# State-space stage of a four-layer network on one core: step sizes replicated over the states by DMA through DRAM instead of TensorE, inputs' replicas three pairs deep, joint product with B

## The chip, the core and the metric

One core of a Trainium2 chip runs the whole program. Its engines are TensorE (PE in the profile; PEld is its weight load), VectorE (DVE), ScalarE (ACT), GpSimd (POOL) and SyncE (SP), which here only issues DMAs. SBUF has 128 partitions, PSUM 8 banks of 512 f32 columns; 16 DMA engines move data between DRAM and SBUF. The metric is the device time of one execution in microseconds, lower is better.

## The reference

The network has four layers on x of shape (16, 32, 128, 128), f32. The change concerns layer 1, a deformable convolution whose offsets pass through a state-space model ("mamba"), forward and backward over sequences of length L = 128 x 128, for 9 offsets per image:

```
def selective_scan(u, dt, A, Bm, Cm, D):
    dA = jnp.exp(dt[..., None] * A)
    dBu = dt[..., None] * Bm[:, :, None, :] * u[..., None]

    def comb(e1, e2):
        a1, b1 = e1
        a2, b2 = e2
        return (a2 * a1, a2 * b1 + b2)
    _, h = jax.lax.associative_scan(comb, (dA, dBu), axis=1)
    return jnp.einsum('bldn,bln->bld', h, Cm) + u * D
```

Here u has 18 inner channels (D_IN), h 16 states per channel (D_STATE), dt is the softplus of a projection, Bm and Cm are projections of u that all channels share. The result is gated with silu(z) and projected back to 9 rows.

## The kernel before

`program` runs the layers one behind another, each in its own block with its own buffers. `state_space` (L738) works on chunks of 512 time steps (LC). The sequence of one direction and one half of the batch (8 images) is 32 chunks long (NC), so there are N = 128 chunks, i = 0 to 127, one behind another; two buffers alternate (u = i % 2). In a chunk the 18 channels go in 9 pairs, p = 0 to 8. One channel of 8 images with 16 states fills 128 partitions.

For each pair the engines do this:

- PE replicates the step sizes dt (tile `dts`, index 0: 8 rows per channel) over the 16 states with a selection matrix `sl`, into `pr` (`rates_of`, L891), and likewise dt * u (`dts`, index 1) into `pu` (`inputs_of`, L897). Both use 32 rows of the array, the quadrant and half of a channel given by `place` (L724).
- ACT makes the decays `da` = exp(dt * A) from `pr` (`decays`, L1060). `da` has three pairs of buffers; decays run two pairs ahead of the scans.
- DVE multiplies `pu` with B in place (`inputs_by_b`, L1131, one instruction for each channel) and scans: h = da * h + pu, into `hs` (`scans`, L1140). Twice per chunk it adds the skip term (`skip`, L1151).
- POOL keeps the last column as the next chunk's carry and multiplies `hs` with C into `hc` (`outputs`, L1187).
- PE sums `hc` over the states into `py` (`reduce`, L930, and `reduce_previous`, L942).

Between the pairs of chunk i the projections of chunk i + 1 are made: PE writes them into the single bank `pp` (x, z, dt, B, C, and the previous output), ACT takes each out (`gate_x`, `gate_z`, `softplus_parts`, `softplus_logs`, `b_copy`, `c_copy`, `out_copy`). POOL makes the step sizes of chunk i + 1 in `steps` (L1174), the first half (pairs 0 to 4) behind its pair 5 and the second (pairs 5 to 8) behind its pair 7.

The order on each engine is written out by hand, and each engine runs its queue in order. In `replicate` (L916) PE waits for two things before it issues anything: scans two pairs back (`wait_inputs`, L904; `pu` has two pairs of banks) and the decays of the pair ahead (`wait_rates`, L910; `pr` has one pair of banks). Then come the inputs of pair p + 1 and the rates of pair p + 2. SP runs a loop over the chunks (L843): loads of the sequence chunk after next (`load`, six transfers of 72, 24, 48, 48, 24 and 72 rows of 2 KB), the two small tables `al` (`load_rates`), and the store of 72 rows (`store`).

Of the kernel before, what the change touches and what calls it, by code (L numbers as in the profile page):

```python
# [8 lines left out]
P = 128  # L9
# [728 lines left out]
def state_space(nc, seq, w_x, w_z, conv_rows, conv_b, w_dt, dt_rows, dt_b, w_b, w_c, a_log, keeps, d_skip, w_out,  # L738
# [5 lines left out]
    KEEP = D_IN  # L744
    USES = 9
    X0, Z0, X1, Z1, DT0, DT1, BB, CC, OUT = range(USES)
    LAST_OF = {0: 1, 1: 1, 2: 3, 3: 3, 4: 4, 5: 6, 6: 6, 7: 8, 8: 8}

    with ExitStack() as ctx:
# [24 lines left out]
        bs = m.sb("bs", [NB, 2, LC])  # L774
        cs = m.sb("cs", [NB, 2, LC])
        da = m.sb("da", [NB, 3, 2, LC])
        hs = m.sb("hs", [NB, 3, 2, LC])
# [6 lines left out]
        py = m.bank("py")  # L784
        pr = m.bank("pr", 2)
        pu = m.bank("pu", 4)
        (w_load, w_ready, a_exp, a_ready, pp_full, pp_drained, ab, e3, lg_ready, dt_ready, dtu_ready,
         rates_done, inputs_done, exp_done, dbu_done, scan_done, carry_ready, hc_done, y_done, y1_done, y2_done) = (m.sem(n) for n in (
             "w_load w_ready a_exp a_ready pp_full pp_drained ab e3 lg_ready dt_ready dtu_ready "
             "rates_done inputs_done exp_done dbu_done scan_done carry_ready hc_done y_done y1_done y2_done").split())  # L790
        s_in = [m.sem("s_in0"), m.sem("s_in1")]
        a_in = [m.sem("a_in0"), m.sem("a_in1")]
        stored = [m.sem("stored0"), m.sem("stored1")]
        LOADS = 16 * len(TAP_PARTS)
# [15 lines left out]
        def _(sp):  # L810
# [32 lines left out]
            with sp.Fori(0, N // 2 - 1) as j:  # L843
                for u in range(2):
                    chunk(j * 2 + u, j, u, False)
            store(N - 2, 0, use_of(N - 1, OUT))
            store(N - 1, 1, use_of(N, 0))
            store(N, 0, use_of(N, 1))
# [4 lines left out]
        def _(pe):  # L853
# [36 lines left out]

            def rates_of(i, u, p, part):  # L891
                hf, q, run = place(2 * p + part)
                rows = slice(32 * q, 32 * q + 32)
                pe.matmul(pr[:, LC * part:LC * (part + 1)], sl[rows, run, :], dts[rows, u, hf, 0, :],  # L894
                          start=True, stop=True, tile_position=(32 * q, 0)).then_inc(rates_done, 1)

            def inputs_of(i, u, p, part):  # L897
                hf, q, run = place(2 * p + part)
                rows = slice(32 * q, 32 * q + 32)
                bank = 2 * ((u + p) % 2) + part  # L900
                pe.matmul(pu[:, LC * bank:LC * (bank + 1)], sl[rows, run, :], dts[rows, u, hf, 1, :],  # L901
                          start=True, stop=True, tile_position=(32 * q, 0)).then_inc(inputs_done, 1)

            def wait_inputs(i, p):  # L904

                if p in (0, HALF_PAIRS):
                    pe.wait_ge(dtu_ready, i * 2 + (1 + p // HALF_PAIRS))
                pe.wait_ge(scan_done, i * D_IN + (2 * p + 4))

            def wait_rates(i, p):  # L910

                if p in (0, HALF_PAIRS):
                    pe.wait_ge(dt_ready, i * 2 + (1 + p // HALF_PAIRS))
                pe.wait_ge(exp_done, i * D_IN + (2 * p + 2))

            def replicate(i, u, p, last):  # L916

                ahead = [(i, u, p + k) if p + k < PAIRS else (i + 1, 1 - u, p + k - PAIRS) for k in (1, 2)]
                if not (last and p + 1 >= PAIRS):
                    wait_inputs(ahead[0][0], ahead[0][2])  # L920
                if not (last and p + 2 >= PAIRS):
                    wait_rates(ahead[1][0], ahead[1][2])
                for part in range(2):
                    if not (last and p + 1 >= PAIRS):
                        inputs_of(*ahead[0], part)
                for part in range(2):
                    if not (last and p + 2 >= PAIRS):
                        rates_of(*ahead[1], part)

# [31 lines left out]
            c_proj(0, 0, 2)  # L961
            wait_inputs(0, 0)
            wait_rates(0, 0)
            for part in range(2):
                inputs_of(0, 0, 0, part)
            for part in range(2):
                rates_of(0, 0, 0, part)
            wait_rates(0, 1)
            for part in range(2):
                rates_of(0, 0, 1, part)  # L970

# [39 lines left out]
        def _(act):  # L1011
# [47 lines left out]

            def decays(i, u, p):  # L1060
# [18 lines left out]
            c_copy(0, 0, False, 2)  # L1079
            decays(0, 0, 0)  # L1080
            decays(0, 0, 1)

            def chunk(i, j, u, last):
                n, un, jn = i + 1, 1 - u, j + u
                for p in range(PAIRS):
                    if p + 2 < PAIRS:
                        decays(i, u, p + 2)
                    elif not last:
                        decays(n, un, p + 2 - PAIRS)
                    if not last:  # L1090
# [24 lines left out]
        def _(dve):  # L1115
# [15 lines left out]
            def inputs_by_b(i, u, p):  # L1131
                if p == 0:
                    dve.wait_ge(pp_drained, use_of(i, BB) + 1)
                dve.wait_ge(inputs_done, i * D_IN + (2 * p + 2))
                for part in range(2):
                    bank = 2 * ((u + p) % 2) + part
                    tile = pu[:, LC * bank:LC * (bank + 1)]
                    dve.tensor_tensor(tile, tile, bs[:, u, :], ALU.mult).then_inc(dbu_done, 1)  # L1138

            def scans(i, u, p):  # L1140
# [4 lines left out]
                for part in range(2):  # L1145
                    bank = 2 * ((u + p) % 2) + part
# [1758 lines left out]
```

## Time and profile before

| | us |
|---|---|
| median of 3 runs | 20,994.22 |
| lowest, highest run | 20,714.11, 21,013.87 |
| the profiled execution | 20,821.64 |
| its span, first to last instruction | 20,820.1 |
| busy in the span: PE, DVE, ACT, POOL | 16,358.0, 14,027.1, 12,953.3, 9,553.7 |
| mean granted TensorE clock, share of full speed | 0.855 |

All rows come from the profiled execution. A group of instructions has its line, engine, operation, the tile written and the tiles read, then busy us and mean ns of one, then the engine's idle time just before them with what ended it. In the timeline each row starts with start and duration in us; "x2" are two instructions run together. A DMA queue's row gives packets, MB, and the time its packets took as a share of all 16 engines' time in the stretch; a row of DMA issues gives their count, KB each, and, where the profile has it, us from issue to landing. An f32 matmul stands as two records.

### The profile page before, as it was taken

To read this page: it belongs to the slowest core of one execution; us is meant where nothing else is said; L and a number is where in the kernel's file an instruction comes from. 1 tells how busy PE (TensorE), PEld (TensorE's weight loads), DVE (VectorE), ACT (ScalarE), POOL (GpSimd) and SP (SyncE) were. 2 spreads that over 40 slices of the span, in tenths; PEclk is the share of its full clock that TensorE was granted. 3 is DMA by queue.
4 is the path that set the end of the run, shared out by engine and by line. 5 is a ranking of instruction groups with operands and counts; after the bars stand their busy time and mean duration, and the time that the engine had idled before them with its cause. 6 is when DMAs were issued, how large, how long until landed. Compare 5 with 4: busy or idle time off the path is not lost. (4 is left out here: it accounts for less than half of the span.)

```text
span 20820.1 us, 421401 instructions
## 1 busy us (share of the span) xinstructions
PE 16358.0 (79%) x158640; PEld 6982.2 (34%) x158640; DVE 14027.1 (67%) x13848; ACT 12953.3 (62%) x21322; POOL 9553.7 (46%) x7800
## 2 busy tenths in 40 slices
PE   6888888888845388888888887699989996336997
PEld 2333333333311022222222222355454453004664
DVE  8999999999951377777777775465565566123322
ACT  6899999988943277777777774466666665220101
POOL 5787877877720177777777775011111111000002
PEclk9999999999977688888888888677787788667988
DMA  2000000000049400000000003221112112993333
GB/s 74 12 11 12 11 12 11 12 12 11 12 114 163 113 17 17 17 17 17 17 17 17 17 17 74 32 31 28 31 31 31 29 31 77 186 209 81 79 68 124
DMA packets 1433366, 986.00 MB, mean 47 GB/s; under 512 B 783816, under 2 KB 1296944, under 8 KB 1399864
## 3 DMA queue, kind: packets, MB, share of 16 engines
q1 hardware_dynamic: 1335848, 837.05, 19.7%
q0 software_dynamic: 17408, 67.11, 1.2%
q10 hardware_dynamic: 79056, 66.70, 1.0%
q8 instruction: 793, 12.99, 0.3%
q14 instruction: 261, 2.14, 0.0%
HBM read 759.05 MB, written 211.63 MB: 47 GB/s over the span
## 5 line engine op out<-in xcount | busy, mean ns | idle before, releaser
L270 DVE TENSOR_TENSOR l_mx<-l_p_v,l_puN 128x2048 f32<-128x2048 f32 x2560 | 5635.7, 2281 | 142.4 <-PE l_p_s L485 129.6
L485 PE MATMUL l_p_s<-l_mx,l_w2z 128*32 128x512 f32 x32768 | 3818.9, 610 | 582.5 <-ACT l_mx L397 313.0
L290 POOL TENSOR_TENSOR l_mx<-l_pv,l_puP 128x2048 f32<-128x2048 f32 x1024 | 3715.6, 3645 | 317.9 <-PE l_p_s L485 312.1
L1196 POOL TENSOR_TENSOR l1m_hc<-l1m_hs,l1m_cs 128x512 f32<-128x512 f32 x2304 | 2922.8, 1269 | 8.5 <-DVE l1m_hs L1148 8.1
L1148 DVE TENSOR_TENSOR_SCAN l1m_hs<-l1m_da,l1m_carry,l1m_pu 128x512 f32<-128x512 f32 x2304 | 2824.1, 1268 | 106.1 <-ACT l1m_da L1066 2.2
L1790 ACT ACTIVATE l1d_ab<-l1d_pt 128x1024 f32<-128x1024 f32 x2304 | 2311.9, 1024 | 611.5 <-DVE l1d_hat L1668 305.6
L416 ACT ACTIVATE l_mx<-l_pv,l_puP 128x128 f32<-128x128 f32 x8192 | 2446.8, 393 | 0.8
L1668 DVE TENSOR_SCALAR l1d_hat<-l1d_ab 128x1024 f32<-128x1024 f32 x2304 | 1923.2, 836 | 443.8 <-ACT l1d_ab L1790 321.0
L1138 DVE TENSOR_TENSOR l1m_pu<-l1m_pu,l1m_bs 128x512 f32<-128x512 f32 x2304 | 1477.1, 687 | 1100.9 <-PE l1m_pu L901 1100.9
L1587 PE MATMUL l1d_po<-l1d_hat,l1d_ring 128*32 128x128 f32 x36864 | 1799.7, 322 | 358.7 <-DVE l1d_hat L1668 233.2
L485 PEld LDWEIGHTS l_p_s<-l_mx,l_w2z 128*32 128x32 f32 x32768 | 982.3, 112 | 3017.5 <-issue 1764.6
L397 ACT ACTIVATE l_mx<-l_mx 128x2048 f32<-128x2048 f32 x1024 | 1954.4, 1909 | 50.8 <-POOL l_mx L290 50.4
L1841 POOL TENSOR_TENSOR l1d_res<-l1d_res,l1d_so 128x2048 f32<-128x2048 f32 x32 | 119.4, 3731 | 3951.8 <-DVE l1d_to L1727 3949.5
L1066 ACT ACTIVATE l1m_da<-l1m_pr,l1m_an 128x512 f32<-128x512 f32 x2304 | 1458.9, 684 | 565.3 <-PE l1m_pr L894 399.9
L901 PE MATMUL l1m_pu<-l1m_dts,l1m_sl 32*128 32x512 f32 x4608 | 1416.0, 691 | 480.4 <-ACT l1m_da L1066 470.7
L1569 PE MATMUL l1d_pg<-l1d_wz,l1d_im 32*128 32x288 f32 x5120 | 1472.5, 656 | 22.1 <-DMA l1d_im<-x_after 10.1
L1655 DVE COPY l1d_ring<-l1d_pg 128x288 f32<-128x288 f32 x1280 | 585.7, 458 | 1323.5 <-PE l1d_pg L1569 1321.8
L1587 PEld LDWEIGHTS l1d_po<-l1d_hat,l1d_ring 128*32 128x32 f32 x36864 | 1030.3, 124 | 1262.9 <-issue 807.2
L894 PE MATMUL l1m_pr<-l1m_dts,l1m_sl 32*128 32x512 f32 x4608 | 1403.2, 687 | 2.7 <-ACT l1m_da L1066 2.7
L2064 POOL TENSOR_TENSOR l3a_lm<-l3a_lmask,l3a_ln 128x1320 f32<-128x1320 f32 x16 | 47.8, 2990 | 2381.2 <-ACT l3a_ln L2015 2381.2
L1776 ACT ACTIVATE l1d_ring<-l1d_pg 128x288 f32<-128x288 f32 x1280 | 526.3, 411 | 877.5 <-PE l1d_pg L1569 876.8
L1552 PE MATMUL l1d_pt<-l1d_yt,l1d_rw 32*128 32x512 bf16 x4608 | 1047.5, 450 | 18.8 <-issue 17.2
(330 smaller groups left out, 22896.5 us busy)
## 6 DMA issues: line engine op xcount, KB each, us to landing
n_xt<-x_after SPq DMA_DIRECT2D x48, 2048.0 KB
l1o_img<-x_after SPq DMA_DIRECT2D x32, 2032.0 KB, 17.2
l_img<-x_after SPq DMA_DIRECT2D x32, 2032.0 KB, 16.9
l1m_sq<-seq SPq DMA_DIRECT2D x256, 144.0 KB
n_xt<-in_x_dram SPq DMA_DIRECT2D x16, 2048.0 KB
l_xs<-in_x_dram SPq DMA_DIRECT2D x128, 256.0 KB, 2.9
x_after<-l_ot SPq DMA_DIRECT2D x128, 256.0 KB, 2.4
l1o_img<-x_after SPq DMA_DIRECT2D x16, 2048.0 KB, 16.9
```

The source lines that it names most:

```text
L270: v.tensor_tensor(mx[:, r % QB, :, :, :], columns.unsqueeze(1).broadcast_to([P, 4, G, P]), rows.broadcast_to([P, 4, G, P]), ALU.max).then_ ...
L290: g.tensor_tensor(mx[:, r % QB, :, :, :], pv[:, u, :, :].unsqueeze(1).broadcast_to([P, 4, G, P]), rows.broadcast_to([P, 4, G, P]), ALU.add ...
L397: act.activation(tile, tile, ACT.Relu).then_inc(max_by_g, 1)
L416: ins = act.activation(mx[:, r % QB, q, t, :], pv[:, u, t, :], ACT.Relu, bias=puP[:, u, t, R * q + r:R * q + r + 1])
L485: ins = pe.matmul(p_s[R * q:R * (q + 1), 512 * u:512 * (u + 1)], w2z[:, 31 - r:63 - r], mx[:, r % QB, q, :, :].rearrange("p t v -> p (t v) ...
L1138: dve.tensor_tensor(tile, tile, bs[:, u, :], ALU.mult).then_inc(dbu_done, 1)
L1148: dve.tensor_tensor_scan(hs[:, p % 3, part, :], da[:, p % 3, part, :], pu[:, LC * bank:LC * (bank + 1)], carry[:, u, c:c + 1], ALU.mult, A ...
L1196: g.tensor_tensor(hc[:, (3 * u + p) % 6, part, :], hs[:, p % 3, part, :], cs[:, u, :], ALU.mult).then_inc(hc_done, 1)
L1569: pe.matmul(pg[:, 512 * half_strip:512 * half_strip + KO], im[C * g:C * (g + 1), :, col_at(g, j)], wz[C * g:C * (g + 1), u, :], start=True ...
L1587: ins = pe.matmul(po[C * g:C * (g + 1), 512 * (s % 2):512 * (s % 2) + P], ring[:, (8 * u + s + k) % RING, g, k, :], hat[:, m % 3, n % 2, P ...
L1668: v.tensor_scalar(hat[:, m % 3], ab[:, m % 2], 1.0, 1.0, ALU.min, ALU.subtract).then_inc(hat_done, 1)
L1790: act.activation(ab[:, m % 2].rearrange("p a n -> p (a n)"), pt[:, 1024 * (m % 2):1024 * (m % 2 + 1)], ACT.Abs).then_inc(abs_done, 1)
```

## The change

The rates leave PE. SP writes each half of a chunk's step sizes to a DRAM tensor `step_rates` when POOL has them, waits until the write has landed, and issues for each channel one transfer that reads the channel's 8 rows of 2 KB, each 16 times, into the 128 partitions of a slot of `rp`. There are 6 slots of one pair each; a slot is filled again when the decays that read it are done. ACT's decays read `rp` in SBUF instead of `pr` in PSUM. The banks of `pr` go to `pu`, which now holds three pairs; PE issues the inputs of pair p + 2 and waits for scans three pairs back alone. DVE's product with B is one instruction for both channels of a pair, B read twice by a step of 0. SP's loop is written out for all 128 chunks.

```diff
+    SLOTS = 6
+    rates = nc.dram_tensor("step_rates", [2, 2, P, LC], F32).ap()
...
+        rp = m.sb("rp", [NB, SLOTS, 2, LC])
...
-        pr = m.bank("pr", 2)
-        pu = m.bank("pu", 4)
+        pu = m.bank("pu", 6)
...
+            def write_steps(n, un, hf):
+
+                sp.wait_ge(dt_ready, n * 2 + (hf + 1))
+                sp.dma_start(rates[un, hf], dts[:, un, hf, 0, :]).then_inc(rates_out, 16)
+                sp.wait_ge(rates_out, n * 32 + (16 * hf + 16))
+
+            def replicas(un, p):
+
+                slot = (3 * un + p) % SLOTS
+                for part in range(2):
+                    hf, q, run = place(2 * p + part)
+                    first = 32 * q + HB * run
+                    sp.dma_start(rp[:, slot, part, :], rates[un, hf, first:first + HB].unsqueeze(1).broadcast_to([HB, D_STATE, LC])
+                                 ).then_inc(rep_in[slot], 16)
+
...
-            def chunk(i, j, u, last):
-
-                sp.wait_ge(pp_drained, use_of(i, Z1) + 1)
-                load(i + 2, u)
-                sp.wait_ge(carry_ready, i * D_IN + D_IN)
-                load_rates(i + 2, u)
-                store(i, u, use_of(i + 1, OUT))
...
+            for hf in range(2):
+                write_steps(0, 0, hf)
+            for p in range(SLOTS):
+                replicas(0, p)
+
+            def chunk(i, u, more, last):
+                for p in range(PAIRS):
+                    q = p + SLOTS
+                    if q < PAIRS or not last:
+                        sp.wait_ge(exp_done, i * D_IN + (2 * p + 4))
+                    if q < PAIRS:
+                        replicas(u, q)
+                    elif not last:
+                        if q - PAIRS in (0, HALF_PAIRS):
+                            write_steps(i + 1, 1 - u, (q - PAIRS) // HALF_PAIRS)
+                        replicas(1 - u, q - PAIRS)
+                    if p == 2 and more:
+                        sp.wait_ge(pp_drained, use_of(i, Z1) + 1)
+                        load(i + 2, u)
+                if more:
+                    sp.wait_ge(carry_ready, i * D_IN + D_IN)
+                    load_rates(i + 2, u)
+                store(i, u, use_of(N, 0) if last else use_of(i + 1, OUT))
+
+            for i in range(N):
+                chunk(i, i % 2, i < N - 2, i == N - 1)
...
-                bank = 2 * ((u + p) % 2) + part
+                bank = 2 * (p % 3) + part
...
-                pe.wait_ge(scan_done, i * D_IN + (2 * p + 4))
...
-                pe.wait_ge(exp_done, i * D_IN + (2 * p + 2))
+                pe.wait_ge(scan_done, i * D_IN + (2 * p + 2))
...
+                ahead = (i, u, p + 2) if p + 2 < PAIRS else (i + 1, 1 - u, p + 2 - PAIRS)
                 if not (last and p + 2 >= PAIRS):
-                    wait_rates(ahead[1][0], ahead[1][2])
...
+                    wait_inputs(ahead[0], ahead[2])
+                    for part in range(2):
+                        inputs_of(*ahead, part)
...
-                act.wait_ge(rates_done, i * D_IN + (2 * p + 2))
+                slot, uses = (3 * u + p) % SLOTS, (PAIRS * u + p) // SLOTS
+                act.wait_ge(rep_in[slot], (j + carried) * (32 * 3) + 32 * (uses + 1))
                 act.wait_ge(scan_done, i * D_IN + (2 * p + 2))
                 for part in range(2):
-                    act.activation(da[:, p % 3, part, :], pr[:, LC * part:LC * (part + 1)], ACT.Exp,
+                    act.activation(da[:, p % 3, part, :], rp[:, slot, part, :], ACT.Exp,
...
-                for part in range(2):
-                    bank = 2 * ((u + p) % 2) + part
-                    tile = pu[:, LC * bank:LC * (bank + 1)]
-                    dve.tensor_tensor(tile, tile, bs[:, u, :], ALU.mult).then_inc(dbu_done, 1)
+                tile = pu[:, 2 * LC * (p % 3):2 * LC * (p % 3 + 1)].rearrange("p (part t) -> p part t", part=2)
+                dve.tensor_tensor(tile, tile, bs[:, u, :].unsqueeze(1).broadcast_to([NB, 2, LC]), ALU.mult).then_inc(dbu_done, 2)
```

In SP's queue the end of one chunk of the loop stood like this before; the rows without "DMA" set registers or wait (`l1m_sq` are the loads of the sequence, `l1m_al` the small tables, `mixed` the store).

```order
L821 DMA l1m_sq<-seq 24x512
L821 ISA
L821 DMA l1m_sq<-seq 72x512
L839 ISA
L824 ISA
L824 DMA l1m_al<-in_a_log_dram 128x18
L825 REGISTER_ALU
L825 DMA l1m_al<-in_keeps_dram 128x1
L828 ISA
L829 ISA
L829 DMA mixed<-l1m_osb 72x512
```

One chunk of SP's queue now, in the written-out program; `step_rates<-l1m_dts` is a write, `l1m_rp<-step_rates` a replica's transfer.

```order
L847 DMA l1m_rp<-step_rates 128x1x512 x6
L825 DMA l1m_sq<-seq 72x512
L825 DMA l1m_sq<-seq 24x512
L825 DMA l1m_sq<-seq 48x512 x2
L825 DMA l1m_sq<-seq 24x512
L825 DMA l1m_sq<-seq 72x512
L838 DMA step_rates<-l1m_dts 128x512
L847 DMA l1m_rp<-step_rates 128x1x512 x10
L838 DMA step_rates<-l1m_dts 128x512
L847 DMA l1m_rp<-step_rates 128x1x512 x2
L828 DMA l1m_al<-in_a_log_dram 128x18
L829 DMA l1m_al<-in_keeps_dram 128x1
```

The replicas of pairs 6 to 8 of chunk i now stand ahead of the loads, the first write and the replicas of pairs 0 to 4 of chunk i + 1 behind them, then the second write, pair 5's replicas and what SP did before at the chunk's end.

On PE, around the first pairs of a chunk, before (`l1m_pu` are the inputs, `l1m_pr` the rates, `l1m_pp` the projections, `l1m_py` the sums over the states):

```order
L861 MATMUL l1m_pp<-l1m_sq,l1m_wtap 128x512 x3
L908 REGISTER_ALU
L901 MATMUL l1m_pu<-l1m_dts,l1m_sl 128x512 x2
L894 MATMUL l1m_pr<-l1m_dts,l1m_sl 128x512 x2
L946 MATMUL l1m_py<-l1m_hc,l1m_slt 32x512 x4
L856 REGISTER_ALU
L866 MATMUL l1m_pp<-l1m_sq,l1m_wz 128x512
```

The same place now:

```order
L892 MATMUL l1m_pp<-l1m_sq,l1m_wtap 128x512 x3
L933 REGISTER_ALU
L926 MATMUL l1m_pu<-l1m_dts,l1m_sl 128x512 x2
L959 MATMUL l1m_py<-l1m_hc,l1m_slt 32x512 x4
L887 REGISTER_ALU
L897 MATMUL l1m_pp<-l1m_sq,l1m_wz 128x512
```

The rates are gone; the inputs stand at the same place but belong to one pair later, and the wait for ACT's decays that stood ahead of them has gone with the rates.

## Rows read from the trace of the kernel before

**Rows 1.** Stretches: busy time by engine, 4000 us of the state-space stage.
```profile
core 0: us, PE busy (x) PEld busy (x) DVE busy (x) ACT busy (x) POOL busy (x), PEclk, DMA share, GB/s
8000.00:12000.00 4000.00, 3463.36 (x13245) 1058.58 (x13244) 3157.86 (x3493) 2820.50 (x3770) 2972.62 (x3863) 0.87 0.06 17
```

**Rows 2.** Groups by line, same 4000 us: busy us, mean ns, idle before.
```profile
L1138 DVE TENSOR_TENSOR l1m_pu<-l1m_pu,l1m_bs 128x512 f32<-128x512 f32 x1654 | 1060.4, 687 | 762.2 <-PE l1m_pu L901 762.2
L1066 ACT ACTIVATE l1m_da<-l1m_pr,l1m_an 128x512 f32<-128x512 f32 x1654 | 1047.3, 684 | 394.2 <-PE l1m_pr L894 273.5 <-DVE l1m_hs L1148 117.2
...
L1155 DVE SCALAR_TENSOR_TENSOR l1m_y<-l1m_xi,l1m_cols,l1m_py 128x512 f32<-128x512 f32 x184 | 132.8, 722 | 0.0
```

**Rows 3.** Timeline, pair 7 of a chunk: start, duration, engine, line, idle before.
```profile
10007.54 1.06 ACT L1043 ACTIVATE l1m_lg<-l1m_ex 128x1024 f32<-128x1024 f32 x1
...
10008.67 1.27 POOL L1176 TENSOR_TENSOR l1m_dts<-l1m_rl,l1m_lg 128x512 f32<-128x512 f32 x1 [1.34 <-ACT l1m_lg L1043]
...
10009.91 1.27 ACT L1066 ACTIVATE l1m_da<-l1m_pr,l1m_an 128x512 f32<-128x512 f32 x2
...
10011.32 0.70 PE L901 MATMUL l1m_pu<-l1m_dts,l1m_sl 32*128 32x512 f32 x2 [1.66 <-ACT l1m_da L1066]
...
10011.33 0.70 PE L894 MATMUL l1m_pr<-l1m_dts,l1m_sl 32*128 32x512 f32 x2
...
10012.49 1.30 DVE L1138 TENSOR_TENSOR l1m_pu<-l1m_pu,l1m_bs 128x512 f32<-128x512 f32 x2 [2.52 <-PE l1m_pu L901]
...
10016.36 1.27 ACT L1066 ACTIVATE l1m_da<-l1m_pr,l1m_an 128x512 f32<-128x512 f32 x2 [1.27 <-DVE l1m_hs L1148]
```

**Rows 4.** DMA, same 4000 us: packets, queue, issues (KB, us to landing).
```profile
DMA packets 68080, 68.77 MB, mean 17 GB/s; under 512 B 34960, under 2 KB 34960, under 8 KB 68080
...
q1 hardware_dynamic: 68080, 68.77, 6.5%
...
l1m_sq<-seq SPq DMA_DIRECT2D x184, 144.0 KB
...
l1m_al<-in_a_log_dram SPq DMA_DIRECT2D x92, 9.0 KB, 2.0
```

**Rows 5.** DMA, an earlier stage: 9-row transfers of 16 KB rows, queued.
```profile
q1 hardware_dynamic: 118, 0.98, 56.9%
...
l1s_shifts<-offsets SPq DMA_DIRECT2D x15, 144.0 KB
```

**Rows 6.** DMA, a later stage: 72-row transfers, 2 KB packets, queued.
```profile
DMA packets 1562, 2.88 MB, mean 180 GB/s; under 512 B 157, under 2 KB 157, under 8 KB 1562
...
q1 hardware_dynamic: 1562, 2.88, 76.9%
```

**Rows 7.** DMA, one chunk's loads in the state-space stage, 3.5 us.
```profile
DMA packets 393, 0.64 MB, mean 183 GB/s; under 512 B 80, under 2 KB 80, under 8 KB 393
...
q1 hardware_dynamic: 393, 0.64, 61.9%
```

**Rows 8.** DMA, the 3.2 us behind it, mostly small packets.
```profile
q1 hardware_dynamic: 326, 0.06, 9.5%
```

**Rows 9.** DMA, norm table's loads: 16 KB to each of 128 partitions.
```profile
DMA packets 1010, 14.71 MB, mean 327 GB/s; under 512 B 112, under 2 KB 112, under 8 KB 112
...
q1 hardware_dynamic: 1010, 14.71, 88.5%
```

**Rows 10.** DMA, convolution's loads to 32 partitions at a time, 100 us.
```profile
q1 hardware_dynamic: 17706, 16.12, 106.9%
```

**Rows 11.** Line L1996: ns min/median/max of one issue on SP.
```profile
L1996 SPq DMA_DIRECT2D pooled<-l3a_po x128: 549/600/1970, 19020.5 to 20157.2; - x128
```

**Rows 12.** DMA issues of the whole span: KB each, us to landing.
```profile
l_xs<-in_x_dram SPq DMA_DIRECT2D x128, 256.0 KB, 2.9
x_after<-l_ot SPq DMA_DIRECT2D x128, 256.0 KB, 2.4
```

More of the change, by code:

```diff
@@ L784, in state_space @@
         py = m.bank("py")
-        pr = m.bank("pr", 2)
-        pu = m.bank("pu", 4)
+        pu = m.bank("pu", 6)
         (w_load, w_ready, a_exp, a_ready, pp_full, pp_drained, ab, e3, lg_ready, dt_ready, dtu_ready,
-         rates_done, inputs_done, exp_done, dbu_done, scan_done, carry_ready, hc_done, y_done, y1_done, y2_done) = (m.sem(n) for n in (
+         inputs_done, exp_done, dbu_done, scan_done, carry_ready, hc_done, y_done, y1_done, y2_done) = (m.sem(n) for n in (
              "w_load w_ready a_exp a_ready pp_full pp_drained ab e3 lg_ready dt_ready dtu_ready "
-             "rates_done inputs_done exp_done dbu_done scan_done carry_ready hc_done y_done y1_done y2_done").split())
+             "inputs_done exp_done dbu_done scan_done carry_ready hc_done y_done y1_done y2_done").split())
         s_in = [m.sem("s_in0"), m.sem("s_in1")]
         a_in = [m.sem("a_in0"), m.sem("a_in1")]
+        rates_out = m.sem("rates_out")
+        rep_in = [m.sem(f"rep_in{n}") for n in range(SLOTS)]
         stored = [m.sem("stored0"), m.sem("stored1")]
@@ L833, in _ @@
                 load_rates(n, n)
-            def chunk(i, j, u, last):
-                sp.wait_ge(pp_drained, use_of(i, Z1) + 1)
-                load(i + 2, u)
-                sp.wait_ge(carry_ready, i * D_IN + D_IN)
-                load_rates(i + 2, u)
-                store(i, u, use_of(i + 1, OUT))
[L843 to L847, printed above, removed]
+            for hf in range(2):
[22 more added lines that the diff above has]
+                chunk(i, i % 2, i < N - 2, i == N - 1)
             store(N, 0, use_of(N, 1))
@@ L889, in out_proj @@
                 both_halves(pp[0:R, :], lambda hi: wo[:, hi, :], y2).then_inc(pp_full, 1)
[L891 to L895, printed above, removed]
             def inputs_of(i, u, p, part):
@@ L907, in wait_inputs @@
                     pe.wait_ge(dtu_ready, i * 2 + (1 + p // HALF_PAIRS))
-                pe.wait_ge(scan_done, i * D_IN + (2 * p + 4))
-            def wait_rates(i, p):
-                if p in (0, HALF_PAIRS):
-                    pe.wait_ge(dt_ready, i * 2 + (1 + p // HALF_PAIRS))
-                pe.wait_ge(exp_done, i * D_IN + (2 * p + 2))
+                pe.wait_ge(scan_done, i * D_IN + (2 * p + 2))
             def replicate(i, u, p, last):
-                ahead = [(i, u, p + k) if p + k < PAIRS else (i + 1, 1 - u, p + k - PAIRS) for k in (1, 2)]
-                if not (last and p + 1 >= PAIRS):
-                    wait_inputs(ahead[0][0], ahead[0][2])
+                ahead = (i, u, p + 2) if p + 2 < PAIRS else (i + 1, 1 - u, p + 2 - PAIRS)
                 if not (last and p + 2 >= PAIRS):
-                    wait_rates(ahead[1][0], ahead[1][2])
-                for part in range(2):
[L924 to L928, printed above, removed]
+                    wait_inputs(ahead[0], ahead[2])
+                    for part in range(2):
+                        inputs_of(*ahead, part)
             def reduce(i, u, pairs):
@@ L961, in _ @@
             c_proj(0, 0, 2)
[L962 to L970, printed above, removed]
+            for p in range(2):
+                wait_inputs(0, p)
+                for part in range(2):
+                    inputs_of(0, 0, p, part)
             def chunk(i, j, u, last):
@@ L1058, in out_copy, with decays @@
                 act.activation(osb[:, u, :], pp[0:R, :], ACT.Copy).then_inc(pp_drained, 1)
-            def decays(i, u, p):
+            def decays(i, j, u, p, carried=0):
                 if p == 0:
                     act.wait_ge(a_ready, i + 1)
-                act.wait_ge(rates_done, i * D_IN + (2 * p + 2))
+                slot, uses = (3 * u + p) % SLOTS, (PAIRS * u + p) // SLOTS
+                act.wait_ge(rep_in[slot], (j + carried) * (32 * 3) + 32 * (uses + 1))
                 act.wait_ge(scan_done, i * D_IN + (2 * p + 2))
                 for part in range(2):
-                    act.activation(da[:, p % 3, part, :], pr[:, LC * part:LC * (part + 1)], ACT.Exp,
+                    act.activation(da[:, p % 3, part, :], rp[:, slot, part, :], ACT.Exp,
                                    scale=an[:, u, 2 * p + part:2 * p + part + 1]).then_inc(exp_done, 1)
@@ L1079, in _ @@
             c_copy(0, 0, False, 2)
-            decays(0, 0, 0)
-            decays(0, 0, 1)
+            decays(0, 0, 0, 0)
+            decays(0, 0, 0, 1)
             def chunk(i, j, u, last):
@@ L1086, in chunk @@
                     if p + 2 < PAIRS:
-                        decays(i, u, p + 2)
+                        decays(i, j, u, p + 2)
                     elif not last:
-                        decays(n, un, p + 2 - PAIRS)
+                        decays(n, j, un, p + 2 - PAIRS, u)
                     if not last:
@@ L1134, in inputs_by_b @@
                 dve.wait_ge(inputs_done, i * D_IN + (2 * p + 2))
-                for part in range(2):
-                    bank = 2 * ((u + p) % 2) + part
-                    tile = pu[:, LC * bank:LC * (bank + 1)]
-                    dve.tensor_tensor(tile, tile, bs[:, u, :], ALU.mult).then_inc(dbu_done, 1)
+                tile = pu[:, 2 * LC * (p % 3):2 * LC * (p % 3 + 1)].rearrange("p (part t) -> p part t", part=2)
+                dve.tensor_tensor(tile, tile, bs[:, u, :].unsqueeze(1).broadcast_to([NB, 2, LC]), ALU.mult).then_inc(dbu_done, 2)
             def scans(i, u, p):
@@ L1145, in scans @@
                 for part in range(2):
-                    bank = 2 * ((u + p) % 2) + part
+                    bank = 2 * (p % 3) + part
                     c = 2 * p + part
```

## The prediction

> **What bounds the kernel now.** The change lies in the state-space stage, so I looked for that stage's period first. The busy time by stretches gives for 4000 us in its middle DVE 3157.86, PE 3463.36, ACT 2820.50 and POOL 2972.62 us, with the DMA engines busy 6% [rows 1]. The groups by line have the skip (L1155) 184 times there [rows 2]; a chunk has two, so 92 chunks ran, 43.5 us each, and the 128 chunks are 5566 us of the 20,820. Per chunk DVE is busy 34.3 us, PE 37.6, POOL 32.3, ACT 30.7. No engine is full. DVE's missing 9 us are named in one row: the product with B (L1138) waited 762.2 us for PE's inputs, 8.3 us per chunk [rows 2]. The timeline shows why [rows 3]: ACT is late with a pair's decays after the softplus logs (table load, then decays at 10009.91); PE issues that pair's inputs only together with the later pair's rates, which wait for those decays (it starts at 10011.32, having waited 1.66 for ACT), and DVE's product starts at 10012.49, 2.52 us idle. So DVE is held by PE, which is held by ACT, through a coupling that is only in PE's order.
>
> **What the change takes away.** Inputs are issued two pairs ahead into three pairs of banks and wait for a scan alone; the rates leave PE. So the 8.3 us per chunk in front of L1138 can go. The rates' matmuls themselves give little: L894 runs beside L901 (both 0.70 us, starting 0.01 apart, [rows 3]), on other rows of the array; I put them at nothing, hidden by L901, with at most 1 us per pair where they run alone. The joint product makes one instruction of two that take 0.69 us each [rows 2] (a pair of them is 1.30 end to end in [rows 3]); its gain is between nothing and 0.6 us per pair, and I take 0.1, 0.9 us per chunk. The decays read SBUF instead of PSUM: 684 ns now [rows 2], no row of that shape from SBUF; an SBUF row of twice the length, L1043, takes 1.06 us [rows 3], so 0.53 to 0.68, 0 to 2.8 us per chunk on ACT, which has 13 us of idle time: nothing. With every wait for PE gone, DVE's own floor is 34.3 - 0.9 = 33.4 us, POOL's 32.3, PE's some 36.
>
> **What it adds.** Per chunk 2 writes of 128 rows of 2 KB to DRAM and 18 replica transfers of 128 packets of 2 KB. The stage now moves 68.77 MB in 92 chunks: 0.75 MB each, of which 360 packets are of 2 KB (33,120 of them in all) [rows 4]. The change moves 5.2 MB more. On 16 engines that would be a moderate load; the question is on how many it runs. A replica's source is 8 rows, each read 16 times, its target 128 partitions. Two stretches where transfers queue without a gap show how the number of engines follows the outer count: transfers of 9 rows keep 56.9% of 16 engines busy, 9.1 engines [rows 5]; transfers of 72 rows 76.9%, 12.3 [rows 6] (12 is the largest divisor of 72 up to 16). By that pattern the replicas run on 8 engines, always the same, if the source's 8 counts; no row shows a source and a target with different outer counts below 16.
>
> The Trainium skill says which one counts: "DMA: Bandwidth & Descriptors", section "Why a DMA increments its semaphore by 16 and not by 1", takes the largest number up to 16 that divides the outer dimension of both sides, and its "Rules for kernel authors" warn of outer dimensions under 16. By that rule it is 8 here; rows 5 and 6 agree with it.
>
> So each of 8 engines carries 288 replica packets per chunk. What does one cost? The stage's own loads, six transfers at a time, are busy 61.9% of 16 engines for 3.5 us with 313 large packets [rows 7]: 34.7 us, less 80 small packets at about 15 ns (4.9 us for 326 mostly small ones, [rows 8]), so 107 ns. Where 2 KB packets queue without a gap it is 76.9% of 16 x 16 us = 196.9 us, less 157 small ones, over 1405 packets: 138 ns [rows 6]. Ends farther off: 16 KB packets to all 128 partitions, 88.5% of 16 x 45 us over 898 packets, 709 ns, which is 89 ns per 2 KB [rows 9]; and transfers to 32 partitions with all engines busy, 16.12 MB in 100 us, 10 GB/s an engine, 203 ns per 2 KB [rows 10]. I take 138: a replica queue of ten transfers is the queue of rows 6, not the short burst of rows 7.
>
> **The sum.** Per chunk, on the 8 engines: replicas 288 x 138 ns = 39.7 us. Other 2 KB packets on the same engines: 22 of the loads, 6 of the store, 2 x 8 of the new writes, 44 x 107 ns = 4.7 us; small ones 0.4 us. Then two stretches in which these engines stand still. SP waits after each write until it has landed before it issues the replicas that read it. The first write also waits for POOL's step sizes, which come out of ACT's logs behind the decays of pair 6; the second is issued behind the replicas of pairs 0 to 4 and must drain behind them, and what is queued behind it on SP (the replicas of pairs 5 to 8, the next loads, the store) waits too. A standstill is one write's tail and one read's head, about one small transfer from issue to landing, 2.0 us [rows 4], plus one replica's issue on SP: its nearest kin (128 packets, source and target cut differently) takes 0.6 us [rows 11]. 2 x 2.6 = 5.2 us. Sum 50.0 us against 43.5. SP itself has 18 x 0.6 us and the rest of some 5 us to issue, no bound.
>
> That is 6.5 us x 128 = +830 us on the profiled execution's 20,822 us (its span and 1.5 us around it): 21,650. The profiled execution lies 172 us under the median of the runs shown, so I put the time at 21,700. DVE then waits for ACT, and ACT for the replicas.
>
> The bounds: at 89 ns 25.6 + 10.3 = 35.9 us, where the engines of the first paragraph bound again (next part); at 203 ns 68.8 us, +3,240 us, 24,060. The period equals today's at 115 ns; it is 2% of the kernel shorter at 104 ns (40.2 us) and longer at 127 ns (46.8 us). From 2% on a difference counts as one here.
>
> **Rivals.** First, DMA doesn't bound (the replicas spread over 16 engines, or packets stay near 90 ns). For it: rows 9, and a stage whose DMA is idle 94% of the time. Against it: rows 5 and 6. Then the way back through DRAM is a latency, not a load. In the timeline POOL's steps are ready at 10009.94 (10008.67 + 1.27) and the pair that needs them has its decays at 10016.36 [rows 3]; write and read of 256 KB now take 2.4 and 2.9 us [rows 12], with SP's issues about 6.9 us, so ready at 10016.8, 0.5 us late; once the 2.5 us idle before it are gone, some 3 us late, partly covered since decays run two pairs ahead. PE's 36 us or DVE's 33.4 plus 0 to 5 us: I take 36. 7.5 x 128 = 960 us saved, 19,860 (35 to 39 us: 19,730 to 20,250). It decides wherever a packet costs under 104 ns on 8 engines.
>
> Second, 8 engines, but at the 107 ns of the stage's own loads: 30.8 + 4.7 + 0.4 + 5.2 = 41.1 us, -2.4 x 128 = -310, 20,510: the gain of the first paragraph is eaten and the time stays within 2%. For it: the same kind of packet in the same stage. Against it: those loads never queue for long.
>
> Third, reading 8 rows 16 times each is slower than reading 128 different rows: no row shows that, and it would lie on the forecast's side, up to the 203 ns end.
>
> **Chances.** DMA-bound above 127 ns, third rival included: 0.48. Second rival (104 to 127 ns): 0.20. First: 0.32. The forecast's own range is 21,240 (127 ns) to 22,700 (166 ns). Cases of both signs hold much of the chance, so the range runs from 19,900, inside the first rival, to 22,700.
>
> **What would show it.** Right: in the stage the DMA share rises from 6% to near 50% (8 of 16 engines), ACT's idle time before its decays ends on a DMA, DVE's wait for PE before the product is gone and one before the scans stands in its place, the period is near 50 us. The engine count is wrong if the share goes well over 50% in any stretch, or if it is low and the period still falls to 36. The packet price is read from the share: 8 engines' time over 332 packets per chunk. The two standstills show as gaps in the DMA row of the timeline, one behind each write. I am wrong altogether if the period falls to 36 us and DVE or PE stands full.

## The result, and the profile after

Slower: 21,673.56 us (median; 21,598.33 to 21,711.89) against 20,955.86, ratio 1.0361, interval 1.0286 to 1.0435. In the profiled executions the stage's scans run from 7213.7 to 13407.6 us, 48.4 us for each of the 128 chunks; before it was 7185.3 to 12748.5, 43.5 us. That is 631 of the 777 us between the two profiles; 118 lie behind the last scan. The forecast was 21,700 and 50.0 us per chunk. The time is near; the reason given for it holds only in part.

The runs below are compared by this period and by their ratio to before, since one profile (sixteen engines, span 22,096.4) ran the stage behind this one at a granted clock of 0.50 and its whole time says nothing.

The busy time by stretches of the changed kernel: the stretch of [rows 1], then parts of one chunk in steps of 6 us, with two steps of 2 us (start of columns: PE, PEld, DVE, ACT, POOL busy; at the end the granted clock, the share of 16 DMA engines, GB/s):

```profile
8000.00:12000.00 4000.00, 3399.56 (x8870) 990.17 (x8868) 2775.16 (x2384) 2556.95 (x3372) 2641.87 (x3454) 0.77 0.35 123
...
10006.00:10008.00 2.00, 1.82 (x4) 0.68 (x4) 2.00 (x2) 1.35 (x3) 2.00 (x3) 1.00 0.06 10
...
10010.00:10016.00 6.00, 4.20 (x16) 1.09 (x12) 5.76 (x6) 2.87 (x5) 5.92 (x7) 1.00 0.58 217
10016.00:10022.00 6.00, 5.58 (x20) 1.81 (x20) 5.82 (x6) 4.30 (x6) 1.71 (x2) 1.00 0.51 194
...
10022.00:10024.00 2.00, 1.50 (x6) 0.30 (x4) 2.00 (x3) 1.97 (x4) 0.00 (x0) 1.00 0.04 16
...
10028.00:10034.00 6.00, 4.90 (x6) 1.26 (x5) 1.04 (x1) 2.87 (x5) 4.01 (x6) 0.50 0.67 222
10034.00:10040.00 6.00, 3.80 (x7) 1.24 (x7) 5.91 (x6) 1.88 (x2) 6.00 (x10) 0.50 0.43 164
10040.00:10046.00 6.00, 5.84 (x13) 1.75 (x14) 4.69 (x5) 3.92 (x7) 6.00 (x9) 0.77 0.00 0
10046.00:10052.00 6.00, 6.00 (x30) 1.72 (x30) 3.54 (x4) 5.94 (x7) 3.01 (x5) 1.00 0.00 0
```

Every engine does less than in [rows 1], and DMA is busy 35%, not the 50% of eight full engines. Where little but replicas runs (10016 to 10022) the share is 0.51: eight engines, full as long as the burst lasts. They stand still for near 2 us behind each write (0.06 from 10006 to 10008, 0.04 from 10022 to 10024), and a third time for some 13 us, until the next write at 10051.90. So over a whole chunk nothing is full; something goes round. The groups by line (as [rows 2]) and the waits of the same 4000 us name it (a wait's row: us in total, times, longest):

```profile
L1155 DVE TENSOR_TENSOR_SCAN l1m_hs<-l1m_da,l1m_carry,l1m_pu 128x512 f32<-128x512 f32 x1479 | 1812.8, 1267 | 864.2 <-POOL l1m_carry L1200 583.0 <-ACT l1m_da L1075 238.9
L1145 DVE TENSOR_TENSOR l1m_pu<-l1m_pu,l1m_bs 128x1024 f32<-128x1024 f32 x740 | 898.4, 1214 | 56.4 <-PE l1m_pu L926 55.6
...
L1075 ACT ACTIVATE l1m_da<-l1m_rp,l1m_an 128x512 f32<-128x512 f32 x1479 | 985.3, 714 | 460.0 <-DMA l1m_rp<-step_rates 408.0 <-DVE l1m_hs L1155 48.0
```
```profile
POOL l1m_carry L1200 <- DMA l1m_al<-in_keeps_dram: 1019.7, 83, 14.9
DVE l1m_hs L1155 <- POOL l1m_carry L1200: 583.0, 83, 9.9
...
ACT l1m_da L1075 <- DMA l1m_rp<-step_rates: 408.0, 224, 5.2
...
ACT l1m_sz L1038 <- POOL l1m_y L1189: 320.5, 66, 5.7
...
SPq L837 <- POOL l1m_dts L1183: 1621.5, 82, 21.5
SPq L847 <- DMA step_rates<-l1m_dts: 911.5, 164, 12.5
```

The wait for PE before the product fell from 762.2 us [rows 2] to 55.6, as forecast. The largest wait of a computing engine is one that the forecast did not name: POOL's first carry of a chunk waits 12.3 us for `al`, a table of 9 KB and a column of 0.5 KB. Why it is late stands in SP's queue, one chunk of the timeline (start, duration from first to last issue, operation, count):

```profile
10004.44 0.34 SPq L838 DMA_DIRECT2D step_rates<-l1m_dts  x1
10006.44 6.34 SPq L847 DMA_DIRECT2D l1m_rp<-step_rates  x10
10012.87 0.77 SPq L838 DMA_DIRECT2D step_rates<-l1m_dts  x1
10022.87 1.21 SPq L847 DMA_DIRECT2D l1m_rp<-step_rates  x2
10024.12 0.46 SPq L828 DMA_DIRECT2D l1m_al<-in_a_log_dram  x1
10024.62 0.43 SPq L829 DMA_DIRECT2D l1m_al<-in_keeps_dram  x1
...
10051.90 0.34 SPq L838 DMA_DIRECT2D step_rates<-l1m_dts  x1
```

The second write is issued at 10012.87 behind ten replicas; it has landed at 10022.87, and only then do the tables go out. The rest of the circle, from POOL, ACT and PE (idle time before, and its releaser, in brackets):

```profile
10029.99 0.19 POOL L1200 TENSOR_TENSOR l1m_carry<-l1m_hs,l1m_al 128x1 f32<-128x1 f32 x1 [12.29 <-DMA l1m_al<-in_keeps_dram]
...
10036.80 1.26 POOL L1189 TENSOR_TENSOR l1m_y<-l1m_y,l1m_sz 128x512 f32<-128x512 f32 x1
...
10038.10 0.60 ACT L1038 ACTIVATE l1m_sz<-l1m_pp 128x512 f32<-128x512 f32 x1 [5.68 <-POOL l1m_y L1189]
...
10038.75 3.78 PE L901 MATMUL l1m_pp<-l1m_xi,l1m_wdtm 128*128 128x512 f32 x4 [2.20 <-ACT l1m_sz L1038]
...
10049.42 1.06 ACT L1051 ACTIVATE l1m_lg<-l1m_ex 128x1024 f32<-128x1024 f32 x1
...
10050.56 1.27 POOL L1183 TENSOR_TENSOR l1m_dts<-l1m_rl,l1m_lg 128x512 f32<-128x512 f32 x1 [2.92 <-ACT l1m_lg L1051]
```

POOL starts late, so its gated product is late, so ACT cannot overwrite the gate `sz`, so the bank `pp` that holds the gate's projection is not free for the step sizes' projection, so logs, POOL's steps and the next first write are late: 10004.44 to 10051.90, 47.5 us, one period. Below, theory A is the forecast's (eight full engines set the period), theory B this circle. DMA's speed enters B too: the time from the first write to the tables' landing is part of the circle.

### The profile page after: what moved, and what is told of

Read it like the earlier page. It is cut to its first block and busy times, and to the rows that moved or that the text cites. A ratio compares the mean times of both kernels' runs of the same rounds, so it can differ in the third digit from the quotient of the medians.

```text
span 21596.8 us, 410258 instructions
## 1 busy us (share of the span) xinstructions
PE 16923.6 (78%) x154032; PEld 7088.5 (33%) x154032; DVE 13945.7 (65%) x12696; ACT 13005.4 (60%) x21322; POOL 9531.4 (44%) x7800
## 5 line engine op out<-in xcount | busy, mean ns | idle before, releaser
L1594 PE MATMUL l1d_po<-l1d_hat,l1d_ring 128*32 128x128 f32 x36864 | 1861.8, 331 | 337.7 <-DVE l1d_hat L1675 218.1
L1075 ACT ACTIVATE l1m_da<-l1m_rp,l1m_an 128x512 f32<-128x512 f32 x2304 | 1534.8, 714 | 728.8 <-DMA l1m_rp<-step_rates 633.8
L892 PE MATMUL l1m_pp<-l1m_sq,l1m_wtap 96*128 96x512 f32 x1536 | 1194.5, 939 | 494.6 <-ACT l1m_osb L1066 325.5
L926 PE MATMUL l1m_pu<-l1m_dts,l1m_sl 32*128 32x512 f32 x4608 | 1547.9, 753 | 18.4 <-DVE l1m_hs L1155 18.4
L1145 DVE TENSOR_TENSOR l1m_pu<-l1m_pu,l1m_bs 128x1024 f32<-128x1024 f32 x1152 | 1398.4, 1214 | 116.1 <-PE l1m_pu L926 114.6
L1200 POOL TENSOR_TENSOR l1m_carry<-l1m_hs,l1m_al 128x1 f32<-128x1 f32 x2286 | 432.5, 189 | 1566.8 <-DMA l1m_al<-in_keeps_dram 1548.8
## 6 DMA issues: line engine op xcount, KB each, us to landing
l_img<-x_after SPq DMA_DIRECT2D x32, 2032.0 KB, 17.1
```

The costliest lines, as they stand in the source:

```text
L1075: act.activation(da[:, p % 3, part, :], rp[:, slot, part, :], ACT.Exp, scale=an[:, u, 2 * p + part:2 * p + part + 1]).then_inc(exp_done, 1)
L1594: ins = pe.matmul(po[C * g:C * (g + 1), 512 * (s % 2):512 * (s % 2) + P], ring[:, (8 * u + s + k) % RING, g, k, :], hat[:, m % 3, n % 2, P ...
```

## The experiments

The edits are shown shortened.

**Tables early (e1).** The two small loads are issued with the sequence loads:

```diff
                         load(i + 2, u)
-                if more:
-                    sp.wait_ge(carry_ready, i * D_IN + D_IN)
-                    load_rates(i + 2, u)
+                        sp.wait_ge(carry_ready, i * D_IN + D_IN)
+                        load_rates(i + 2, u)
```

> The changed kernel, but the small tables of the next chunk but one (al and the KEEP column) are issued on SP beside the sequence loads, ahead of the second write, instead of behind it. Theory A (the forecast's: eight engines full of 138 ns packets): the traffic is the same, so the period stays at 48.5 us and the time at 21,650 (within 150). Theory B (packets of some 91 ns, engines with room, SP's order is the bound: the tables stand behind the second write's wait, POOL's first carry waits 12.3 us per chunk for them): POOL's wait for al falls to nothing, DVE's wait for POOL before the scans with it, period 41 to 43 us, time 20,750 to 21,000.

Ratio 1.0192 (1.0125 to 1.0259), 45.7 us. The wait for `al` is gone from the waits. The same bytes per chunk take 2.7 us less: theory A falls. But B's 41 to 43 was too low: ACT now waits 463.4 us in the window for replicas (5.3 per chunk) and DVE's wait for PE, 512.4 us, is back:

```profile
L1144 DVE TENSOR_TENSOR l1m_pu<-l1m_pu,l1m_bs 128x1024 f32<-128x1024 f32 x786 | 956.2, 1217 | 512.4 <-PE l1m_pu L925 512.4
```

**Sixteen engines (e2), and both (e3).** Each row goes to DRAM twice, so that a replica reads 16 rows:

```diff
-dts[:, un, hf, 0, :]                                 # write, 128 rows
+dts[:, un, hf, 0, :].unsqueeze(1).broadcast_to([P, 2, LC])
-rates[un, hf, first:first + HB].unsqueeze(1).broadcast_to([HB, D_STATE, LC])
+rates[un, hf, first:first + HB].rearrange("h c t -> (h c) t").unsqueeze(1).broadcast_to([2 * HB, D_STATE // 2, LC])
```

> The changed kernel, but every row of step sizes is written twice to DRAM, so that a replica's source has 16 rows, each read 8 times, instead of 8 rows read 16 times; order and waits as in the changed kernel. Theory A (8 engines full): the load spreads over 16 engines, period 36 to 41 us, 20,000 to 20,700. Theory B (SP's order): only the drain of the ten replicas ahead of the second write shortens, from 10 us to some 5, the tables come 5 us earlier, period 43 to 45 us, 20,950 to 21,250, POOL still waits some 6 us per chunk for al. If the outer count does not set the number of engines: no change, 21,650, and bursts of replicas keep the same share of the engines busy.

> Both edits of the first two runs together on the changed kernel: small tables early, replicas on 16 engines. Load theory (what is left is what the engines carry): the gain is that of the 16 engines over the early tables alone, 5 us per chunk or more, period under 41 us, under 20,700. Latency theory (a chunk's decays wait for logs, steps, write and read in a loop over ACT, and the two edits each take a part of that way): the two gains of 2.9 and 5.1 us overlap, since both bring the tables forward; period 41.5 to 43 us, 20,750 to 20,950.

e2: 1.0057 (1.0021 to 1.0092), 43.6 us. e3: 1.0091 (1.0018 to 1.0163), 43.7 us. In e2's burst of replicas the share is 0.95, against 0.51:

```profile
10032.00:10036.00 4.00, 4.00 (x18) 1.03 (x15) 3.72 (x4) 1.33 (x2) 3.92 (x5) 1.00 0.95 263
```

The gains do not add, as the latency theory had it, but the period is above its 41.5 to 43: in e2 POOL still waits 681.7 us for the tables, e3 takes that wait away, and the period stays. Both stand at before's 43.5 us. It is not what the DMA engines carry that holds the period there, since e8 below moves the same bytes per chunk in 37.6 us.

**The trip alone (e9).** Before, with the step sizes sent to DRAM and the first pair's replicas read back into a tile that nobody reads; ACT also waits for them:

```diff
+round_trip(i + 1, 1 - u, hf)      # SP: wait steps, write, wait, read two replicas
 act.wait_ge(rates_done, i * D_IN + (2 * p + 2))
+act.wait_ge(rep_in[p // HALF_PAIRS], i * 32 + 32)      # p in (0, HALF_PAIRS)
```

> The kernel before with the trip through DRAM as a delay alone: SP writes each half of the step sizes to DRAM, waits for it, reads the first pair's two replicas of that half back into a tile that nothing reads, and ACT's decays of pairs 0 and 5 also wait for them; the rates still come from TensorE, and the small tables and loads stand ahead of it on SP. Traffic added: 1.5 MB per chunk in place of 5.2. Latency theory: the decays of pair 0 come some 5 us later, of which up to 2.5 us are covered by decays that run two pairs ahead; period 45 to 48 us, 21,050 to 21,500. Load theory: a third of the traffic, DMA engines over 85% idle, period within 1 us of before, 20,850 to 21,000.

0.9951 (0.9888 to 1.0014), 42.4 us: the latency is there (ACT waits 184.5 us for the read, 2.0 per chunk) and the period is no longer. The pure latency theory falls too (45 to 48). What is left is the burst of ten replicas in front of everything else, in the changed kernel 16.4 us from 10006.44 to 10022.87; no run takes the burst alone away, but e2 shortens it and gains 4.8 us per chunk.

**Before with PE uncoupled (e4), and with the joint product (e5).**

```diff
-    wait_inputs(...); wait_rates(...); inputs_of x2; rates_of x2
+    wait_inputs(...); inputs_of x2; wait_rates(...); rates_of x2
```
```diff
-for part in range(2): dve.tensor_tensor(tile, tile, bs[:, u, :], ALU.mult)
+dve.tensor_tensor(both, both, bs[:, u, :].unsqueeze(1).broadcast_to([NB, 2, LC]), ALU.mult)
```

> The kernel before, but PE issues a pair's inputs before it waits for the decays that free the later pair's rates (one wait moved behind two matmuls). Reading of the forecast (DVE is held by PE only through this order): DVE's 762 us of waiting before L1138 fall to under 100, period 36 to 40 us, 19,900 to 20,400. Rival (DVE then waits the same time for ACT's decays before the scans): the wait moves to L1155's successor line, period 42 to 43.5 us, 20,650 to 20,900.

> The kernel before, with the joint product alone: one tensor_tensor over two banks of PSUM with B broadcast over them, in place of two. By the forecast's term (0.1 us per pair saved, and DVE waits for PE anyway): period 42.6 to 43.5 us, time 20,700 to 20,900, not told apart from before. Rival (fixed cost of an instruction is the larger part of 0.69 us): 1.0 us for the joint product, 0.4 us per pair saved, still behind PE's wait, at most 460 us.

e4: 0.9963 (0.9929 to 0.9996), 42.4 us; DVE still waits 674.1 us for PE. The 1.1 us are not shown to come from the edit: e9, which only adds work, also has 42.4 us, and in both the mean granted clock of the stage is higher than in before (0.91 and 0.92 against 0.87). e5: 1.0027 (0.9994 to 1.0060), 43.5 us; the joint product takes 1217 ns for 2 x 687, and DVE's wait grows from 762 to 822. So my reading of before was wrong: DVE is not held by the order of inputs and rates. In e4 PE issues the inputs behind two projections that wait for ACT:

```profile
10026.16 2.84 PE L861 MATMUL l1m_pp<-l1m_sq,l1m_wtap 96*128 96x512 f32 x6 [0.78 <-ACT l1m_sz L1028]
10031.09 2.02 PE L866 MATMUL l1m_pp<-l1m_sq,l1m_wz 96*128 96x512 f32 x2 [2.09 <-ACT l1m_xi L1022]
10033.04 1.22 PE L901 MATMUL l1m_pu<-l1m_dts,l1m_sl 32*128 32x512 f32 x2
```

All nine projections of a chunk go through the one bank `pp`, each waiting until ACT has drained the last.

**The freed banks for `pp` (e7), with sixteen engines (e8).** e1 (e3 for e8), with three banks for `pp` in turn, and inputs one pair ahead in four banks, as before:

```diff
-pp = m.bank("pp");     pu = m.bank("pu", 6)
+pp = m.bank("pp", 3);  pu = m.bank("pu", 4)
-pe.wait_ge(pp_drained, use_of(n, what))
+pe.wait_ge(pp_drained, use_of(n, what) - (1 if what == DT0 else 2))
```

> The changed kernel with the early tables, and with the two banks of PSUM that the rates gave up spent otherwise: the projections' tile pp gets three banks in turn in place of one (PE waits for the drain two uses back, except for the first step-size projection, which needs the gate), inputs one pair ahead in two pairs of banks, as in the kernel before. If the loop over PE's and ACT's hand-over of the one bank pp sets when the logs come: PE's waits for ACT before pp fall from some 9 us per chunk to under 2, the logs and with them the replicas come earlier; period 38 to 42 us, 20,150 to 20,650. If the loop is the trip through DRAM alone: period 45 to 46 us, 21,250 to 21,400.

> The same with the replicas on 16 engines too. If both hand-over and trip lie in one loop: 36 to 39 us, 19,900 to 20,300, and DVE or POOL is the busiest engine, over 85% busy. If the load of DMA is what is left: a gain over the run with 8 engines of 4 us per chunk or more; if latency, of 1 to 2.

e7: 0.9852 (0.9788 to 0.9916), 40.2 us. e8: 0.9724 (0.9654 to 0.9794), 37.6 us, DVE 90% and POOL 86% busy:

```profile
8000.00:12000.00 4000.00, 3548.26 (x11468) 1081.01 (x11468) 3586.43 (x3086) 3254.25 (x4337) 3423.16 (x4449) 0.94 0.60 172
```

e8 beats both kernels. e7 against e1 is worth 5.5 us per chunk, although its inputs are less deep: the hand-over of `pp` holds the period once the tables are early, unless part of the gain is the clock's, 0.81 in e1 and 0.90 in e7 (next part). The sign promised for it came only in part: in e7 PE still waits 464.9 us in front of a projection for ACT, 4.7 per chunk, not under 2. In before, where all eight banks are taken, it could not be tried alone; that it sets the 43.5 us there is read from e4's rows and not shown.

**PE's order and clock (f1, f2, f3).** The granted clock falls to 0.50 once per chunk: in the table above it is 0.50 from 10028 to 10040. f1 is e1 with pair 5's inputs between the projections of pair 2; f2 adds to f1 repeated matmuls at pair 2; f3 adds some to e8:

```diff
     if p == 2 and not last: x_proj(n, un, 1)
+    if p == 2: replicate(i, u, 3, last)      # f2: pair 4's inputs three times, pair 5's twice
     if p == 2 and not last: z_proj(n, un, 1)
```

> The changed kernel with the early tables, and one move in PE's order: the inputs of pair 5 are issued between the two projections at pair 2 instead of behind them. Order theory (DVE's wait for pair 5's inputs, 5.9 us per chunk, costs because PE issues them behind projections that wait for ACT): that wait falls under 1 us, period 42 to 44.5 us, 20,900 to 21,150. Clock theory (the time lies on the chain from projection to projection, of which 10 to 15 us per chunk run at a granted clock of 0.50): DVE's wait only moves to a later pair, period 45 to 46 us, 21,250 to 21,400.

> The same with three idle stretches of PE partly filled: at pair 2 the inputs of pairs 4 and 5 are computed three times and twice into the same banks, only the last time announced; 6 matmuls of 0.56 us each that change no value. Clock theory: the granted clock stays at 1.00 over the projections at pair 2 (5.49 us at half clock falls to 2.84), the mean clock in the stage rises from 0.81 to over 0.90, period 2 to 5 us shorter than in the run before, 250 to 650 us. Without that: the added 3.4 us of matmuls lie in waits or lengthen them, 0 to +2 us per chunk.

> The run with three banks for the projections, early tables and 16 engines, and the inputs of pair 4 computed three times, in the 2.9 us in which PE waits for the gate before the step sizes' projection. Clock theory: the step sizes' projections (2.94 and 3.37 us) take 1.98 each, mean clock in the stage from 0.94 to over 0.97, period 1 to 2.5 us shorter than 37.6, 130 to 320 us off 20,290. Otherwise no change or up to 100 us slower.

f1: 1.0231 (1.0180 to 1.0282), 46.5 us, not the order theory's 42 to 44.5; DVE's wait moves to ACT's decays (528.6 us). f2: 1.0435 (1.0382 to 1.0488), 49.4 us: mean clock 0.77, and pair 4's six matmuls run at half speed (5.49 us). f3: 0.9668 (0.9621 to 0.9716), 37.4 us: 0.2 us per chunk, not told apart from e8. The clock theory is neither confirmed nor refuted, since neither run raised the clock: in f2 it was at 0.50 already when the added matmuls began, and they only lengthened the chain; in f3 it is 0.94 as in e8.

The clock stays a rival for a part of every difference here. Over all the profiles period and mean granted clock of the stage go together: 37.4 and 37.6 us at 0.94, 42.4 (e4, e9) at 0.91 and 0.92, 43.5 to 43.7 at 0.86 and 0.87, 45.7 to 49.4 at 0.77 to 0.81. Which of the two leads is not shown. The clock alone does not make the differences: e1 at 0.81 is 2.7 us faster than g1 (below) at 0.80, and e7 at 0.90 is 2.2 us faster than e9 at 0.92.

**Writes from POOL's queue (g1).** Base: the changed kernel.

```diff
-sp.dma_start(rates[un, hf], dts[:, un, hf, 0, :]).then_inc(rates_out, 16)
+g.dma_start(rates[un, hf], dts[:, un, hf, 0, :]).then_inc(rates_out[hf], 16)   # behind POOL's steps
```

> The changed kernel with both writes of the step sizes issued by POOL, behind its second step product, on a queue of their own; SP only waits for them and keeps its order (tables still behind the second wait). Queue theory (the second write takes 10 us because it stands behind ten replicas in SP's queue): from POOL's issue to landing it takes 2 to 5 us, SP's wait for it falls by 5 us or more, replicas of pairs 5 on and the small tables come that much earlier, POOL's wait for al falls from 12.3 to under 7 us per chunk, period 45 to 47 us, 21,150 to 21,450, against a first write that is some 1.3 to 2.5 us later. Engine theory (it waits because the eight engines are busy with replicas, whatever the queue): the second write still takes 8 us or more, period 48.5 to 50.5 us, 21,600 to 21,900.

1.0374 (1.0327 to 1.0421), 48.4 us: no change. The first write of a chunk lands 2.3 us after POOL issues it, the second, with replicas under way, some 6 us after (6.2 in the chunk shown), in place of 10.0. So about 4 us of the 10.0 were the place in SP's queue; the rest stays on a queue of its own too, while the eight engines are busy. POOL's wait for `al` falls from 1019.7 to 704.3 us, but the replicas still drain on eight engines, and ACT waits 585.5 us for them instead of 408.0. The write's time lies between the two expectations, the period is the second's.

```profile
step_rates<-l1m_dts POOLq DMA_DIRECT2D x1, 256.0 KB, 2.3
...
step_rates<-l1m_dts POOLq DMA_DIRECT2D x1, 256.0 KB, 6.2
...
POOL l1m_carry L1199 <- DMA l1m_al<-in_keeps_dram: 704.3, 81, 10.4
ACT l1m_da L1073 <- DMA l1m_rp<-step_rates: 585.5, 229, 6.9
```

## Why the prediction was right in the number and wrong in the reason

- **Eight engines: right.** 0.51 in the burst, 0.95 with 16 source rows. The Trainium skill ("DMA: Bandwidth & Descriptors", "Why a DMA increments its semaphore by 16 and not by 1") says so, and the trace agrees.
- **138 ns per packet: wrong, a term mis-sized.** The rows below give 35.3% of 16 x 4000 us; less 45,986 small packets at 15 ns, over 240,621 large ones, that is 91 ns. The replicas' term is 288 x 91 = 26.2 us, not 39.7. With sixteen engines the same sum gives 109 ns. The estimate of 150 ns from the Trainium skill's port rule ("SBUF — State Buffer", "Door 1: The DMA port swizzle") does not hold here; whether two engines met at one port at all, no run shows.

```profile
DMA packets 286627, 493.86 MB, mean 123 GB/s; under 512 B 45986, under 2 KB 45986, under 8 KB 286607
...
q1 hardware_dynamic: 286607, 493.70, 35.3%
```

- **Two standstills of 2.6 us: near; a third left out, the step that failed.** The eight engines stand still near 2 us behind each write, about as priced. The forecast says that the first write also waits for POOL's step sizes, and gives this wait no time: the engines then stand still some 13 us per chunk (SP waits 1621.5 us in the window for the step sizes), while the circle goes through POOL, ACT and PE. A whole chunk is one chain, not a full queue with two gaps. What ties the burst into it is the second write: SP waits 10.0 us for it, and behind it stand the small tables, for which POOL was waiting and which the forecast's list of what is queued there does not have. The replicas' term was 13.5 us too large, and what is not transfer 48.4 - 26.2 - 5.1 = 17.1 us (near 2 + 2 + 13) in place of 5.2, 11.9 too small: two errors that nearly cancel, and by luck 50.0 came near 48.4. With 91 ns put into the forecast's own sum the period would be some 36 us, the first rival's.
- **DVE's wait for PE: right as an observation** (762.2 to 55.6), wrong as a gain. In e4 the coupling is gone and the period falls by 1.1 us at most, not 8. The inputs' wait looks like the mark of the chain over `pp` (read from e4's rows): a buffer in front of it took the mark away, not the chain. The first rival's 36 us rested on the same reading; e8 nears it, only with three banks for `pp`.
- **The small terms.** Joint product: forecast 0.1 us per pair, measured 1374 to 1217 ns and no time (e5). Replica's issue: 0.6 us, measured 0.58. Decays from SBUF: forecast 0.53 to 0.68, measured 714 ns against 684, outside the range, 0.5 us per chunk on ACT. The profiled execution's distance to the median: the forecast names 172 us and adds 50; with all of it the forecast would be 21,820.
- **The signs.** Promised: ACT waits for DMA (408.0 us, yes), a wait before the scans in place of PE's (864.2 us, yes, but mostly for POOL), a share near 50% (no, 35 over the stage; 0.51 only within the burst, more only beside loads and writes, which use more engines), gaps behind each write (yes). The share of the whole stage alone would have told full engines from a circle.
- **Open:** how much of the 2.6 us between e7 and e8 is the shorter burst and how much the clock (0.90 and 0.94) was not separated. Of the 777 us, 146 lie outside the chunks, 118 of them behind the last scan. There the same instructions kept PE busy 6341.54 us in place of 6211.11, at a granted clock of 0.77 in place of 0.79; that the change caused this is not shown.

## What to carry to other kernels

When an engine's queue gets a wait in the middle, list everything behind it by who consumes it: here 9.5 KB of tables behind a burst cost 2.7 us per chunk. A stage in which no engine is full can be a circle; find the hand-over that closes it (here one PSUM bank for nine projections) before moving work around it, and spend freed room there. Here the trip through DRAM cost by what was queued with it, more than by the share of busy engines or by its latency alone.

## What the runs showed of the hardware

- In both kernels the granted clock falls to 0.50 (1.2 GHz) once per chunk, behind waits of PE around pair 2 (PE was busy 1.89 of 4 us from 10028 to 10032 in before, 0.12 of 2 us from 10024 to 10026 in the changed kernel), and a projection of 2.84 us takes 5.49. With the rates' 18 matmuls of a chunk gone and PE waiting more, the stage's mean went from 0.87 to 0.77: an estimate from these means and the periods is 11 us per chunk at 0.50 before and 22 after. The matmuls added in f2 did not raise it. The first row is from before, the second from the changed kernel:

```profile
10031.25 5.49 PE L861 MATMUL l1m_pp<-l1m_sq,l1m_wtap 96*128 96x512 f32 x6 [0.68 <-ACT l1m_sz L1030]
...
10025.88 5.49 PE L892 MATMUL l1m_pp<-l1m_sq,l1m_wtap 96*128 96x512 f32 x6 [2.37 <-ACT l1m_sz L1038]
```

- ACT reads 512 columns from SBUF no faster than from PSUM: 714 against 684 ns.
- Eight engines against sixteen (e2): the mean packet goes from 91 to 109 ns, by which the doubled engines would bring 1.7 times the rate; in the two bursts shown it is 263 against 194 GB/s, 1.4 times.
- A write of 256 KB landed after 2.0 us with nothing ahead of it, after 10.0 behind ten replicas in the same queue, and after some 6 us from another engine's queue beside them (g1).
